# A three-layer decoder kernel on one core: ten buffers for the gathered expert results, two sums per tile step, and the softmax weights' transposes moved to the end of their steps

## What is computed

```python
x = x + attn(_layernorm(x), ...)            # 16 heads of 16, rotary, per-head norm, softmax
x = x + xattn(_layernorm(x), ctx_512, ...)  # 16 heads, latent keys of 64 numbers, softmax
x = x + ffn(_layernorm(x), Wr, Wg, Wu, Wd)  # 8 experts, each row goes to its top 2

probs = softmax(x @ Wr); topk_w, topk_idx = top_k(probs, 2); topk_w /= sum(topk_w)
for i in range(8):
    h = silu(x @ Wg[i]) * (x @ Wu[i])
    output += w_i * (h @ Wd[i])
```

## Time and profile before

| | us |
|---|---|
| median of 3 runs | 677.04 (676.82 to 677.63) |
| the profiled execution's own time | 674.06 |
| its span, first to last instruction | 672.3 |
| PE busy | 601.7 (89%), mean granted clock 0.961 |
| DVE busy | 498.5 (74%) |
| ACT busy | 339.6 (51%) |
| POOL busy | 250.2 (37%) |

### The profile page before, as it was taken

How to read it: one execution, slowest core, us unless ns; L and a number is a source line. 1 busy time by engine, 2 the same in 40 slices (tenths; PEclk the granted TensorE clock), 3 DMA queues, 4 the chain that set the end, 5 groups by cost and what they waited for, 6 DMA issues and landing times.

```text
span 672.3 us, 14930 instructions
## 1 busy us (share of the span) xinstructions
PE 601.7 (89%) x5522; PEld 452.4 (67%) x5522; DVE 498.5 (74%) x1197; ACT 339.6 (51%) x1178; POOL 250.2 (37%) x226
## 2 busy tenths in 40 slices
PE   2786989998899999999999999999988888899980
PEld 1465777777778766676766766767655677788860
DVE  3899799998366797737987489874798877655574
ACT  1277899999573024741157212671238735455540
POOL 2104000000003853833447734667346413734330
PEclk9897999998799999999999999999997999999995
DMA  8599990000000000000000120002127212433366
GB/s 285 167 338 338 335 319 3 2 2 1 1 2 17 17 0 3 2 1 17 1 1 2 64 63 1 2 1 71 42 81 235 64 48 78 145 108 98 112 217 221
DMA packets 40679, 58.96 MB, mean 88 GB/s; under 512 B 15040, under 2 KB 35136, under 8 KB 39968
## 3 DMA queue, kind: packets, MB, share of 16 engines
q1 hardware_dynamic: 35536, 47.25, 22.8%
q0 software_dynamic: 3408, 9.34, 3.8%
q10 hardware_dynamic: 1664, 1.41, 0.7%
HBM read 46.56 MB, written 29.40 MB: 113 GB/s over the span
## 4 chain that ended last, share of the span: by engine, by line
PE 66%; DVE 18%; ACT 9%; issue 4%; DMA 3%; ACTq 0%; SPq 0%; DVEq 0%
PE bank L378 57%; PE bank L387 9%; ACT ex L1640 2%; ACT kbd L1630 2%; DVE x L1552 2%; DMA lncol<-in_L_attn_ln_kv_b 1%; DVE nmax L1064 1%; DMA gb<-results 1%; DVE wlo L1486 1%; DVE m L1163 1%; DVE yr L1026 1%; DVE hvar L1031 1%; ACT ex L1750 1%; DVE newton L1045 1%; DVE newton L1047 1%
## 5 line engine op out<-in xcount | busy, mean ns | idle before, releaser
L1898 POOL TENSOR_TENSOR r<-m,m 128x512 f32<-128x512 f32 x80 | 104.5, 1331 | 101.6 <-DVE m L1163 87.7
L1163 DVE TENSOR_TENSOR m<-bank,cst 128x512 f32<-128x512 f32 x192 | 122.1, 685 | 25.7 <-PE bank L378 21.0
L1750 ACT ACTIVATE ex<-bank,nmax 128x64 f32<-128x64 f32 x256 | 73.4, 341 | 27.7 <-DVE nmax L1452 27.7
L378 PE MATMUL bank<-xth,wbh 128*128 128x512 f32 x192 | 80.0, 417 | 0.0
L378 PE MATMUL bank<-xth,wbl 128*128 128x512 f32 x192 | 75.3, 392 | 0.0
L378 PE MATMUL bank<-xtl,wbh 128*128 128x512 f32 x192 | 75.0, 390 | 0.0
L1733 ACT ACTIVATE qc<-bank 128x512 f32<-128x512 f32 x32 | 17.4, 595 | 98.8 <-PE bank L378 98.8
L378 PE MATMUL bank<-wop,qc 128*128 128x256 f32 x256 | 62.3, 389 | 0.0
L1945 POOL DMA_INDIRECT results<-ys,place x39 | 37.9, 971 | 62.5 <-ACT ys L1825 60.7
L378 PEld LDWEIGHTS bank<-wop,qc 128*128 128x128 f32 x256 | 46.6, 189 | 14.7 <-issue 8.1
L1640 ACT ACTIVATE ex<-bank,nmax 128x64 f32<-128x64 f32 x256 | 54.5, 358 | 2.6 <-DVE nmax L1064 2.5
(11 more groups left out here) (245 smaller groups left out, 1420.7 us busy)
## 6 DMA issues: line engine op xcount, KB each, us to landing
slots<-in_fill SPq DMA_DIRECT2D x1, 17544.0 KB, 65.2
xs<-slots SPq DMA_DIRECT2D x39, 129.0 KB, 2.2
gb<-results SPq DMA_DIRECT2D x16, 256.0 KB, 3.7
wo_s<-in_L_xattn_Wo SPq DMA_DIRECT2D x1, 2048.0 KB, 18.6
wq_s<-in_L_xattn_Wq SPq DMA_DIRECT2D x1, 2048.0 KB, 11.9
wraw<-in_L_ffn_Wg SPq DMA_DIRECT2D x8, 256.0 KB, 3.8
wraw<-in_L_ffn_Wu SPq DMA_DIRECT2D x8, 256.0 KB, 4.0
wraw<-in_L_ffn_Wd SPq DMA_DIRECT2D x8, 256.0 KB, 4.6
```

The costliest lines, as they stand in the source:

```text
L378: return e.matmul(o, l, r, start=start, stop=stop, skip_group_check=True)
L1163: last = e.tensor_tensor(m4[n % 2][m][:, :].rearrange("p (b s) -> p b s", s=S), products[half][:, :].rearrange("p (b s) -> p b s", s=S), t ...
L1750: last = e.activation(ex[b % 4][:, h * 64:(h + 1) * 64], score_banks(b)[odd][:, n * 64:(n + 1) * 64], ACT.Exp, bias=nmax[b % 4][:, 4 * odd ...
L1898: last = e.tensor_tensor(rope[n % 6][half][:, :], m4[n % 2][first][:, :], m4[n % 2][second][:, :], op)
```

## The change

It has two parts that have nothing to do with each other.

**Softmax steps 4, 5 and 6 of every block, on PE.** The first part of the context products now stands ahead of the scores, the second part right behind them, and the transposes last. Nothing is added or removed.

```diff
                 for s in range(12):
                     if 4 <= s < 7:
+                        contexts(blk, s - 4, (0,))
                         cross_scores(blk, s)
-                        contexts(blk, s - 4, (0,))
+                        contexts(blk, s - 4, (1,))
                         cross_weights_T(blk, s - 3)
-                        contexts(blk, s - 4, (1,))
```

```diff
+        pairs = [s7(f"gb{i}", [P, 2, 2, D]) for i in range(5)]
+        pairs.append(Space(nc, mxhat_at)("gb5", [P, 2, 2, D]))
+        s8 = Space(nc, low.at)
+        ones = [s8(f"gb{i}", [P, 1, 2, D]) for i in range(6, 9)]
+        ones.append(Space(nc, mxT_at)("gb9", [P, 1, 2, D]))
+        gb = pairs + ones
+        GB_OF = {t: (t // 2, t % 2) for t in range(4 * EARLY)}
+        GB_OF.update({t: (2 * EARLY + t - 4 * EARLY, 0) for t in range(4 * EARLY, NT)})
...
+        def combined(t):
+            return t - int(t > SUMMED_APART)
...
-        COMBINES = {EARLY_DONE + n: c for n, c in ((5, (0, 1)), (6, (2, 3)), (7, (4, 5)), (8, (6, 7, 8)), (9, (9, 10, 11)))}
+        COMBINE_FROM = EARLY_DONE + 5
+        SUMMED_APART = 4 * EARLY
...
+            def combine(t, k):
+                n, m = GB_OF[t]
+                w.wait_ge(d_gb[n], 16)
+                w.wait_ge(t_comb, 2 * combined(t) + k)
+                e.scalar_tensor_tensor(tile(t), gb[n][:, m, k, :], share[:, t, k:k + 1], tile(t), ALU.mult, ALU.add).then_inc(t_comb, 1)
...
                 if 1 <= i <= tiles:
                     h_low(i - 1)
+                if i >= COMBINE_FROM:
+                    combine(i - COMBINE_FROM, 0)
                 if i + 2 < tiles:
                     x_low(i + 2)
                 if i + 2 < tiles:
                     places(i + 2)
+                if i >= COMBINE_FROM:
+                    combine(i - COMBINE_FROM, 1)
...
-                for t in COMBINES.get(i, ()):
-                    combine(t)
-            for t in range(4 * EARLY, NT):
-                combine(t)
+            for t in range(tiles + 2 - COMBINE_FROM, NT):
+                if t != SUMMED_APART:
+                    for k in range(2):
+                        combine(t, k)
...
+            w.wait_ge(t_comb, 16)
+            e.dma_start(ov[:, 4:8, :], x3[:, 4:8, :]).then_inc(d_out, 16)
+            t = SUMMED_APART
+            for k in range(2):
+                w.wait_ge(d_gb[GB_OF[t][0]], 16)
+                part = gb[GB_OF[t][0]][:, 0, k, :]
+                e.activation(part, part, ACT.Copy, scale=share[:, t, k:k + 1]).then_inc(t_scaled, 1)
+            w.wait_ge(t_comb, 24)
+            e.dma_start(ov[:, 8:12, :], x3[:, 8:12, :]).then_inc(d_out, 16)
+            for t in (13, 15):
+                w.wait_ge(t_comb, 2 * combined(t + 1))
+                e.dma_start(ov[:, t:t + 1, :], x3[:, t:t + 1, :]).then_inc(d_out, 16)
...
+            t = SUMMED_APART
+            for k in range(2):
+                w.wait_ge(t_scaled, k + 1)
+                w.wait_ge(t_summed, k)
+                e.tensor_tensor(tile(t), tile(t), gb[GB_OF[t][0]][:, 0, k, :], ALU.add).then_inc(t_summed, 1)
...
-            for t in range(8):
-                results_load(t)
+            for t in range(0, 4 * EARLY, 2):
+                results_load(t, t + 2)
+            w.wait_ge(t_comb, 8)
             result(0, 4)
-            for t in range(8, 12):
-                results_load(t)
-            result(4, 8)
-            result(8, 12)
-            for t in range(12, NT):
-                results_load(t)
-            for t in range(12, NT):
-                result(t, t + 1)
+            for t in range(4 * EARLY, NT):
+                results_load(t, t + 1)
+            w.wait_ge(t_summed, 2)
+            result(SUMMED_APART, SUMMED_APART + 1)
+            w.wait_ge(t_comb, 2 * combined(15))
+            result(14, 15)
```

More of the change, by code:

```diff
@@ L318, in decoder @@
         d_fill, d_scat = sem("d_fill"), sem("d_scat")
-        d_xs, d_ys, d_gb = ([sem(f"d_{n}{i}") for i in range(k)] for n, k in (("xs", 4), ("ys", YS), ("gb", 4)))
+        d_xs, d_ys, d_gb = ([sem(f"d_{n}{i}") for i in range(k)] for n, k in (("xs", 4), ("ys", YS), ("gb", 10)))
         s_phase = sem("phase")
@@ L390, in decoder @@
         tile = lambda t, n=1: x[:, t * D:(t + n) * D]
+        ov = out.rearrange("b s d -> (b s) d").rearrange("(t p) d -> p t d", p=P)
         x3 = x[:, :].rearrange("p (t d) -> p t d", d=D)
@@ L1546, in h_low @@
                                 ALU.subtract).then_inc(t_hl, 1)
-            def combine(t):
-                for k in range(2):
-                    w.wait_ge(d_gb[t % 4], 16 * (t // 4 + 1))
-                    w.wait_ge(t_comb, 2 * t + k)
-                    e.scalar_tensor_tensor(tile(t), gb[t % 4][:, k, :], share[:, t, k:k + 1], tile(t), ALU.mult, ALU.add).then_inc(t_comb, 1)
+            def combine(t, k):
[3 more added lines that the diff above has]
+                e.scalar_tensor_tensor(tile(t), gb[n][:, m, k, :], share[:, t, k:k + 1], tile(t), ALU.mult, ALU.add).then_inc(t_comb, 1)
             tiles = sum(TILES)
```

16 lines of the change are left out of this document (8 added, 8 removed).

## The result

The changed kernel takes 674.45 us (median of 9 runs, 669.92 to 676.02), the kernel before 677.26 us on the same chip (median of 9, 676.31 to 678.45). The ratio is 0.9946, with a 95% interval of 0.9927 to 0.9965: 3.7 us less, or 2.4 to 4.9. The ratio uses all runs of both kernels; the two medians by themselves are 2.8 us apart. Forecast were 5.8 us less. On a second chip the changed kernel came to 0.9925 (0.9897 to 0.9954), 5.0 us less. One of the 17 runs of the kernel before beside e5 to e8 was slow (712.08 us) and is left out of their ratios.

A forecast was written before the change was run, and what follows sets the result against it. PE was taken to bound cross attention, the round through DVE, ACT and POOL block 3, and DVE with its loads the end. -4.9 - 1.6 + 0.7 = -5.8 us gave 671.2 us from 677.04, range 669.0 to 674.2.

The forecast's parts named there:

- Part 1, the end: Expert loop's last turns, last loads and DVE's last sums: 4.9 us less.
- The loop's part: Last turns of the expert loop: PE waits less for `thl`, so the last `ys` and last store come 2.3 us earlier.
- The tie between DVE's chain and the arrival of tile 13: At the end, DVE's 20 sums finish at 661.6, the same time as tile 13's results arrive; 0.3 us allowed.
- the last results come late: Rival at the end: last store and loads land 2 to 3 us later and DVE waits; 673.5 us, chance 0.12.
- 2.2 us from the last sum to the end: After DVE's last sum at 665.2, the last store takes 2.2 us, so the span ends at 667.4.
- Tile 12 costs nothing: At the end, ACT's copies and POOL's additions for tile 12 are done by 664.5, while DVE works to 665.2.
- Part 2, blocks 0 to 2: Steps 4 to 6: fewer array changes give 2.7 us, new waits in step 6 take 1.1; 1.6 us less.
- the array changes gain nothing: Rival for steps 4 to 6 of blocks 0 to 2: no gain from the new order; 673.4 us, chance 0.15.
- context products at the head hold up every step: Rival: scores wait behind context parts in all 12 steps, up to 0.75 us each; 681.1 us, chance 0.05.
- Part 3, block 3: Steps 4 to 6: scores of step 5 stand behind the waiting context part; 0.7 us more, from 0 to 1.4.
- the clock falls in block 3: Rival: PE's longer pause before step 5 halves the clock, three products cost 1.5 us more; 672.7 us, chance 0.10.
- the likeliest case: The main forecast for the whole kernel: 5.8 us less, 671.2 us, own range 670.0 to 672.5; chance 0.50.

The follow-up runs named there:

- e5: e3 with the last two stores swapped, so SP stores tile 15 and ACT tile 14; ratio 0.9889 to the kernel before.
- e8: e3 with the transposes of steps 4 to 6 of blocks 0 to 2 split into two pairs around the scores; ratio 0.9980 to the kernel before.
- e4: The changed kernel itself, unaltered, run and profiled again on the second chip; ratio 0.9925 to the kernel before.
- e6: e3 with the old table of sums put back; ratio 0.9935 to the kernel before.
- e9: e3 with both sums of tile 12 given to DVE instead of ACT and POOL; ratio 0.9870 to the kernel before.
- e11: e3 with POOL's drain moved ahead of its two additions of tile 12; ratio 0.9868 to the kernel before.
- e3: The changed kernel with block 3 keeping the old order of its steps 4 to 6; ratio 0.9898 to the kernel before.
- e10: e3 with tile 12 summed on DVE and tile 11 on ACT and POOL, the scalings ahead of ACT's store; ratio 0.9867 to the kernel before.

## Why the prediction was right, and where it was off

**Part 1, the end: -4.9 forecast, -4.1 measured (E-F).** The loop's part was forecast at 2.3 us and is 2.7 (last `ys` 9.72 us after E before, 7.03 in e4). Removing the table of sums alone from the change costs 2.2 us (e6). The tie between DVE's chain and the arrival of tile 13 was right: DVE waits for it 0 to 0.6 us in the executions with the changed end and the new table of sums, 0.37 in e4. The 4.05 us of the earlier trace rows were not the first of the four loads, as the working says: tile 12 had landed 3.3 us after the first issue (665.75 against 662.43), and the 4.4 us are tile 13's, for which the sum needed them. In e4 tile 13 lands 5.3 us after the first issue (657.42 against 652.12), so the rival "the last results come late" was right that they land later, but for the kernel it comes to that wait of 0.6 us at most, not to 2.3. The last sum ends 5.2 us earlier against E (24.69 to 19.49), 0.3 more than forecast. The step that failed is "2.2 us from the last sum to the end", together with "Tile 12 costs nothing": it followed POOL's two additions to their end, and not the drain behind them, which in the kernel before was over 8.0 us before the end. It costs 0.7 us against tile 12 on DVE (e9), 0.9 to 1.0 against the same work with the drain ahead of it (e11). The additions' other cost, DVE's longer sums (0.5 us in e4, 0.6 in e3), wasn't in the working either.

**Part 2, blocks 0 to 2: -1.6 forecast, -2.5 measured.** The mechanism and both signs were right; the terms were mis-sized. By block the gain is 0.77, 0.86 and 0.86 us. A pair of array changes costs 0.36 us (e8) rather than 0.3, 3.3 us in nine steps instead of 2.7. The wait in step 6 is 0.28 us net in block 1 (0.85 from `chosen` to the next step against 0.57), and it is as long in block 2 (0.32 on PE in both). In block 0 it is 0.69 (e4), but the kernel before already had a wait in its step 6, which the working didn't count:

```profile
283.65 0.65 PE L378 MATMUL bank<-ssb,kvr 64*64 64x256 f32 x4 [0.42 <-DVE qc L1473]
```

So the new waits are 0.27 + 0.28 + 0.28 = 0.8 us, where 1.1 was forecast, and 3.3 - 0.8 = 2.5 is what was measured. The rival that the array changes gain nothing is out: e8 puts changes in and gets the loss, be it by draining or by lost overlap. The rival that context products at the head hold up every step is out too: in the blocks 0 to 2 PE has no wait but the one ahead of step 6.

**Part 3, block 3: +0.7 forecast, +1.57 measured.** The step named was the right one, the scores of step 5 behind the context part. The maximum of step 5 comes 2.24 us later against that of step 4 (4.71 us after it in e4, 2.47 in e3), where the working had 1.3. That difference of 0.9 us is the low clock by the rows: from the start of the context part to the maximum it is 2.02 us in e4 (508.07 to 510.09), and the working had 0.55 + 0.51 for it. So the rival "the clock falls in block 3" with its 1.5 us was a part of the likeliest case, not a case beside it. The rows at half clock cost 2.57 - 1.42 = 1.15 us on PE up to the transposes. Against C, ACT's next copy of the transposed weights comes 2.36 us later than in e3 (forecast 0.9), and DVE starts the table of the expert tiles 2.13 later; one of the table's first rows is then 0.56 us shorter than in e3 (0.42 against 0.98), for a reason that the rows don't give, and 1.57 are left at the last maximum.

**The sum.** -4.1 - 2.5 - 0.2 + 1.57 - 0.1 = -5.3 us in the traces (the 0.2 and 0.1 belong to no part of the change), forecast -5.8; the errors of the parts, 0.8 and 0.9 us too optimistic and 0.9 too pessimistic, partly cancel. Timed, the gain is 3.7 us on the first chip and 5.0 on the second, with overlapping intervals. On the median of the first runs of before the ratio gives 677.04 x 0.9946 = 673.4 us, inside the range of 669.0 to 674.2 and 0.9 above the likeliest case's own range. By the time alone the forecast wouldn't have been told from its rivals: 673.4 is just what "the order gains nothing" gave, and "the last results come late" gave 673.5. It is the stages that bear the mechanism out, and that the sum of three mis-sized parts came out near is in part luck.

**A better version.** e9 is at 0.9870 (0.9845 to 0.9895), faster than the kernel before by 8.8 us on its chip, where the stages account for 7.5. It wasn't timed side by side with the changed kernel (0.9925 and 0.9946 on other chips); stage by stage it is 2.3 us shorter than e4, 1.57 in block 3 and 0.77 at the end. e10 and e11 can't be told from it by time.

## What to carry to other kernels

Follow each engine's program to its last instruction, drains included, when work is moved to the end of it: a drain on GpSimd that was hidden can become the end of the kernel. Before moving elementwise work from DVE to GpSimd, check whether DVE will run two-input instructions meanwhile; here the move gave nothing back. Grouping matmuls of one tile size pays where PE has no gaps (here 0.36 us a pair of changes), but where PE already waits, keep the instruction that starts the next round early and splits the pause: here one long pause came with the low clock as well.

## What the runs showed of the hardware

- The first drain behind POOL's loop took 6.6 to 8.2 us in every trace: 7.1 to 8.2 directly behind the indirect DMAs, 6.6 behind two additions, whether these started 1.1 us (e10) or 6 to 7 us (e3, e4) after the last indirect DMA's start. A second one, behind the additions of e11, took 1.04. What it waits for isn't shown.
- DVE's sum of 0.485 us took up to 1.26 us beside a POOL addition.
- After a PE pause of 2.0 to 2.2 us the granted clock was 0.50; around pauses of 1.54 and 1.39 us with 0.69 us of work between them it fell to 0.50 too; after pauses of 0.39 and 0.91 us with as much work between them it stayed at 1.00.
- Two executions of one program agree to 0.1 us in most stages behind A, and one of them can lose 4.2 us in an unchanged loop; the time ahead of A varies by 3.8 us.
